# Another order of three engine queues in an attention stage of a fused graph-network kernel

## The reference, cut to what matters

```python
q2 = (q @ wiq.T + biq).reshape(N, H, D).transpose(1, 0, 2)      # N = 384, H = 16, D = 64
scores = jnp.einsum('hnd,hmd->hnm', q2, k2) * scale + mask[None]
attn = jax.nn.softmax(scores, axis=-1)
out = jnp.einsum('hnm,hmd->hnd', attn, v2)
x = x + out.transpose(1, 0, 2).reshape(N, OUT_F) @ wo.T + bo
```

## Time and profile before

| what | us |
|---|---|
| median of 3 runs | 937.59 (937.17, 937.59, 942.64) |
| the profiled execution, own time | 937.65 |
| its span, first to last instruction | 935.9 |
| attention: first transposes of head 0 to first product of the output projection | 225.05 to 295.47 |
| first product of relation 0 starts | 372.02 |
| TensorE's granted clock | 0.999 of full speed |

### The profile page before, as it was taken

How to read it: one execution, slowest core, us unless ns; L and a number is a source line. 1 busy time by engine, 2 the same in 40 slices (tenths; PEclk the granted TensorE clock), 3 DMA queues, 4 the chain that set the end, 5 groups by cost and what they waited for, 6 DMA issues and landing times.

```text
span 935.9 us, 13614 instructions
## 1 busy us (share of the span) xinstructions
PE 913.5 (98%) x4723; PEld 802.7 (86%) x4723; DVE 610.6 (65%) x1003; ACT 361.9 (39%) x568; POOL 489.6 (52%) x436
## 2 busy tenths in 40 slices
PE   5999999998999999999999999999999999999998
PEld 4999999997788887888888888888888888887886
DVE  6998888885886735656656565665646656434645
ACT  6433333344886334232223232323224345233532
POOL 5334444456676454757576575757685601320363
PEclk9999999999999999999999999999999999999999
DMA  8998756571337617453445535344333444333412
GB/s 204 243 278 223 228 155 154 153 195 2 52 43 206 161 20 257 110 171 98 142 114 167 150 113 157 104 149 113 92 110 122 157 130 136 118 107 90 136 45 90
DMA packets 89907, 128.60 MB, mean 137 GB/s; under 512 B 34480, under 2 KB 67456, under 8 KB 89856
## 3 DMA queue, kind: packets, MB, share of 16 engines
q1 hardware_dynamic: 72784, 123.54, 43.4%
q0 software_dynamic: 15552, 0.11, 4.2%
q10 hardware_dynamic: 1520, 4.30, 1.4%
HBM read 117.17 MB, written 7.59 MB: 133 GB/s over the span
## 4 chain that ended last, share of the span: by engine, by line
PE 89%; DMA 3%; DVE 3%; POOL 2%; issue 1%; ACT 1%; POOLq 0%; DVEq 0%; ACTq 0%
PE ps L672 47%; PE ps L471 18%; PE ps L746 8%; PE ps L515 4%; PE ps L635 4%; PE ps L595 2%; PE ps L551 2%; PE ps L538 2%; DMA raw<-in_L_gnn_weight 1%; DMA weight_d<-weight_sum,cell 1%; DVE wlo_all L1372 1%; DMA b_in<-in_L_gnn_biv 1%; PE ps L432 1%; POOL weight_d L1863 1%; POOL mean_lo L1842 1%
## 5 line engine op out<-in xcount | busy, mean ns | idle before, releaser
L1372 DVE TENSOR_TENSOR wlo_all<-raw,whi_all 128x1024 fp32r<-128x1024 f32 x120 | 199.3, 1669 | 121.6 <-ACT whi_all L960 121.5
L471 PE MATMUL ps<-acts,whi_all 128*128 128x384 f32 (+1 forms) x640 | 164.2, 337 | 0.0
L1842 POOL TENSOR_TENSOR mean_lo<-mean_f,mean_hi 128x384 fp32r<-128x384 f32 x76 | 88.6, 1165 | 119.6 <-ACT mean_hi L1110 119.3
L1110 ACT ACTIVATE mean_hi<-mean_f 128x384 fp32r<-128x384 f32 x76 | 39.9, 526 | 272.8 <-DVE mean_f L1539 272.8
L672 PE MATMUL ps<-whi_all,mean_hi 128*128 128x512 f32 x452 | 139.7, 390 | 2.5 <-POOL mean_lo L1842 2.5
L672 PE MATMUL ps<-wlo_all,mean_hi 128*128 128x512 f32 x452 | 139.3, 389 | 0.0
L672 PE MATMUL ps<-whi_all,mean_lo 128*128 128x512 f32 x452 | 139.2, 389 | 0.0
L960 ACT ACTIVATE whi_all<-raw 128x1024 fp32r<-128x1024 f32 x120 | 124.5, 1049 | 24.5 <-PE ps L672 18.0
L471 PEld LDWEIGHTS ps<-acts,whi_all 128*128 128x128 f32 x640 | 117.0, 190 | 0.1
L1863 POOL DMA_INDIRECT weight_d<-weight_sum,cell x48 | 95.5, 1989 | 31.5 <-DMA weight_d<-weight_sum,cell 18.6
L1810 POOL DMA_INDIRECT count_d<-met,cell x48 | 77.6, 1617 | 60.0 <-DMA count_d<-met,cell 46.8
(11 more groups left out here) (209 smaller groups left out, 1718.6 us busy)
## 6 DMA issues: line engine op xcount, KB each, us to landing
raw<-in_L_gnn_weight SPq DMA_DIRECT2D x64, 512.0 KB
rows_b<-rows_d SPq DMA_DIRECT2D x24, 384.0 KB, 5.2
raw<-in_L_gnn_w_gate SPq DMA_DIRECT2D x16, 512.0 KB
raw<-in_L_gnn_W_self SPq DMA_DIRECT2D x16, 512.0 KB
raw<-in_L_gnn_W_neigh SPq DMA_DIRECT2D x16, 512.0 KB
count_d<-total_r SPq DMA_DIRECT2D x8, 576.0 KB
rel_r<-count_d SPq DMA_DIRECT2D x8, 576.0 KB, 4.5
raw<-in_L_gnn_wq SPq DMA_DIRECT2D x32, 128.0 KB
```

The lines of the kernel that those rows point to most:

```text
L471: mm = pe.matmul(ps[:, j % 2, 0:N], stationary[j % RING][:, k, :], acts[:, a, moving, k, :], start=i == 0, stop=i == 3 * KT - 1)
L1110: act.activation(mean_of(q, k, 0)[:, 0, :], sums_of(q, k), ACT.Copy).then_inc(S["mean_hi"], 1)
L1372: dve.tensor_tensor(wlo_row[slot], raw[slot][:, :], whi_row[slot].bitcast(F32), ALU.subtract)\
L1842: pool.tensor_tensor(mean_of(q, k, 1)[:, 0, :], sums_of(q, k), mean_of(q, k, 0)[:, 0, :].bitcast(F32), ALU.subtract).then_inc(S["mean_lo"], 1)
```

## The change

It moves entries in the three hand-written queues and nothing else; no operation is added or removed, and no wait condition is changed. On PE the scores stand at the head of a step, `turn_probs(o, 0)` goes behind the third scores, and `turn_probs(o, 2)` behind `weigh_values(e)`. On ACT the exponentials of the next pair stand between the high copies in smaller groups, and `read_spread` and `pair_high` change places. On DVE the last maxima come earlier and `invert_sums` stands between the low parts. In the last step the tiles of `wo` take the corresponding places.

```diff
@@ -599,30 +599,29 @@
 
             for pair in range(H // 2):
                 e, o = 2 * pair, 2 * pair + 1
-                if pair:
-                    turn_probs(e, 0)
-                    turn_probs(e, 1)
                 if pair and o + 1 < H:
                     scores(pair + 1, 0)
                 if o + 1 < H:
                     scores(pair + 1, 1)
-                if o + 1 == H:
+                else:
                     turn_output(0)
                     turn_output(1)
                 if pair:
+                    turn_probs(e, 0)
+                    turn_probs(e, 1)
                     weigh_values(e - 1)
                 turn_probs(e, 2)
-                turn_probs(o, 0)
                 spread_sums(pair)
                 if o + 1 < H:
                     scores(pair + 1, 2)
                 else:
                     turn_output(2)
+                turn_probs(o, 0)
                 turn_probs(o, 1)
-                turn_probs(o, 2)
                 if o + 1 == H:
                     turn_output(3)
                 weigh_values(e)
+                turn_probs(o, 2)
             weigh_values(H - 1)
 
             def output_blocks(f, nt, blocks):
@@ -1056,27 +1055,28 @@
                 if pair and more:
                     exp(e + 2, 0)
                     exp(o + 2, 0)
+                if not more:
+                    column_high(0)
+                probs_high(e, 2)
                 if more:
                     exp(e + 2, 1)
+                    exp(o + 2, 1)
                 else:
-                    column_high(0)
                     column_high(1)
-                probs_high(e, 2)
                 probs_high(o, 0)
                 if more:
-                    exp(o + 2, 1)
+                    exp(e + 2, 2)
                 else:
                     column_high(2)
                 probs_high(o, 1)
+                if more:
+                    exp(o + 2, 2)
+                else:
+                    column_high(3)
                 probs_high(o, 2)
-                if not more:
-                    column_high(3)
-                if more:
-                    exp(e + 2, 2)
-                    exp(o + 2, 2)
-                read_spread(pair)
                 if pair:
                     pair_high(pair - 1)
+                read_spread(pair)
 
             act.wait_ge(S["probs_turned"], H * NT)
             act.dma_start(xres[:, :, :], x.rearrange("(t p) d -> p t d", p=P)).then_inc(S["x_in"], 16)
@@ -1460,29 +1460,31 @@
                     score_max(e + 2, 1)
                 if pair:
                     probs_low(e, 0)
-                    probs_low(e, 1)
                 if more:
                     score_max(o + 2, 1)
+                if pair:
+                    probs_low(e, 1)
                 if not more:
                     column_low(0)
-                    column_low(1)
                 if pair:
                     make_pair(pair - 1)
                 probs_low(e, 2)
+                if more:
+                    score_max(e + 2, 2)
+                    score_max(o + 2, 2)
+                else:
+                    column_low(1)
                 probs_low(o, 0)
                 if more:
-                    score_max(e + 2, 2)
+                    invert_sums(e + 2)
                 else:
                     column_low(2)
                 probs_low(o, 1)
                 if more:
-                    score_max(o + 2, 2)
+                    invert_sums(o + 2)
+                else:
+                    column_low(3)
                 probs_low(o, 2)
-                if not more:
-                    column_low(3)
-                if more:
-                    invert_sums(e + 2)
-                    invert_sums(o + 2)
 
             def last_pair_low(pair):
                 dve.wait_ge(S["pair_hi"], pair + 1)
```

## The result

The changed kernel takes 934.78 us (median of 20 runs, 932.97 to 936.1), the kernel before beside it 937.19 (20 runs, 936.12 to 943.52): ratio 0.9959, interval 0.9946 to 0.9972. It is about 2.4 us faster, inside the 1% that the prediction called no change, and 0.2 from the predicted 934.6. The profiled execution took 936.0, that is 1.2 above the median and the second longest of the 20, with a span of 934.2.

The account below looks back on a forecast made before the run. It took PE, busy 913.5 of 935.9 us, as the bound, with only idle time to win. Attention ends 2.1 us earlier (1.1 + 3.6 - 2.6); the count chain's advance of 3.0 gives 937.65 - 3.0 = 934.65, so 934.6; range 932.7 to 939.3.

Parts of the forecast that it names:

- The step (8.41 to 7.8): Middle steps 1 to 6 of attention: hidden PE waits go, gaining 0.6 us each, 3.6 us in all.
- The 0.1 for `turn_probs(o, 1)`: Middle steps: a new PE wait before this tile, whose buffer is not yet free, 0.07 to 0.16 us, taken as 0.1.
- The first step (1.1 earlier): First step of attention: the first weighing comes at 230.8 for 231.94, a gain of 1.1 us.
- The last step (15.65): Last weighing of step 6 to output projection: 15.65 us for 13.01, 2.6 lost, with three PE waits.
- The end of attention (293.4): Output projection starts at about 293.4 for 295.47, 2.1 us earlier (1.1 + 3.6 - 2.6).
- if ACT and DVE keep up: Condition for a 7.8 us step: ACT's busy 7.31 and DVE's 7.17 both lie below it.
- The advance of the count chain (S = 3.0): Behind attention: the last count's advance S sets the time won in the end, 3.0 us, between 1.1 and 4.3.
- Counts 30 and 31 fall into its end: Counts meet the end, not the start, of the burst of wo tiles and x reload, landing 3 to 4 us earlier.
- Rival one: Counts follow their own issue, not the burst, so the count chain advances only 1.1 us: 936.5; chance 0.25.
- What PE could use (2.1 + 2.2): Limit on the gain before relation 0: attention's 2.1 us plus PE's 2.2 us wait for the first mean, 4.3.
- Rival two: wo tiles meet counts POOL does not wait for during `pair_low`; count chain advances PE's full 4.3 us: 933.3; chance 0.15.
- Rival three (slower): ACT and DVE do not follow, steps stay 8.4 us, the last step still loses 2.6: 939.1; chance 0.12.

Follow-up runs that it names:

- after_nopair: The changed kernel with POOL's two `pair_low` operations left out for pairs 0 to 5, only the signal kept: 934.98 us, ratio 0.9968.
- early_w: The changed kernel with SP issuing relation 0's first two weight tiles ahead of its wait for the last count: 935.36 us, ratio 0.9959.
- pe_only: The kernel before with PE's new order alone, ACT and DVE keeping their old queues: 941.84 us, ratio 1.0049.
- actdve_only: The kernel before with the new orders of ACT and DVE alone, PE keeping its old queue: 952.42 us, ratio 1.0149.
- old_tail: The changed kernel with the last step of attention in the order of the kernel before on all three engines: 937.29 us, ratio 0.9981.
- new_tail_early: new_tail with SP also issuing relation 0's first two weight tiles ahead of its wait for the last count: 933.26 us, ratio 0.9953.
- before_early: The kernel before with SP issuing relation 0's first two weight tiles ahead of its wait for the last count: 937.53 us, ratio 0.9996.
- before_44: The kernel before with its last four counting transfers left out and not waited for: 937.23 us, ratio 0.9994.
- after_44: The changed kernel with its last four counting transfers left out and not waited for: 935.37 us, ratio 0.998.
- new_tail: The changed kernel with the last step of attention in a third order on PE, ACT and DVE: 939.66 us, ratio 1.001.

## Why the prediction was right, and where it was off

**The step (8.41 to 7.8): right, and a little too careful.** 7.70 to 7.73 in four of six steps, and in all six once POOL is out of the way (after_nopair) or no copy happens to be held (early_w, 7.72 to 7.74). The 0.1 for `turn_probs(o, 1)` did not come. pe_only and actdve_only show that the three orders are needed together.

**The first step (1.1 earlier): right.** From the wait's end at 228.54 to the first weighing at 230.70 it is 2.16, before 231.94 - 228.56 = 3.38: 1.2 won.

**The last step (15.65): right.** 15.46. The three waits were 0.7, 0.6 and 1.5 in the text and 0.74, 0.34 and 1.24 on the chip.

**The end of attention (293.4): off by 1.2.** It came at 294.62, 0.85 earlier than before instead of 2.1. The step that failed is "if ACT and DVE keep up": busy time of 7.17 for DVE was taken as what DVE needs, and a copy that stands still beside POOL's work was not in it. In this execution it cost 0.6 + 1.5 = 2.1 us; without these, attention would have ended near 292.5, and in early_w, which has the same attention and no copy held, it ended at 292.50. So with ACT and DVE keeping up the sum was even a little too careful. Which copies are hit is a matter of phase, that is of where a copy falls against POOL's queue in that execution: the kernel before has the copies elsewhere and was not hit, old_tail was hit lightly, new_tail_early three times.

**The advance of the count chain (S = 3.0): the size is open, the place was wrong.** Between the two profiled executions the tables moved by 0.97, but with the 2.66 by which the chain of after was late ahead of the first `pair_low` it is 3.63. Other profiles agree on the order of size and show the scatter: from count 17 to count 43 it took 91.6 to 95.9 in the three kernels with the old attention and all of `pair_low` (before, before_early, before_44), and 87.6 to 93.0 in the seven with the new steps. What failed is where it was to come from. "Counts 30 and 31 fall into its end" was to give 1.9 or more and gave 0.29: the wo tiles were issued 3.07 earlier (predicted 4.5), the counts 0.55, the reload of x 0.68, the next count 0.84. The stretch from count 17 to 28, priced at 1.1 for `pair_low`'s wait, gave 3.20: that wait of 1.09 is gone, and POOL also waited less for its counts to land (1.07 for 3.79), which the sum had at nothing. Why it waited less is not shown.

The page "DMA: Bandwidth & Descriptors" of the Trainium skill (section Queues, rings and completion order) made the tie to the burst worth nothing, and 0.29 is near that. But its turns packet by packet don't make these counts quick: beside the loads the next one still started 8.11 behind them, where it had been 8.40, and in early_w 5.55. How each transfer shared the DMA engines no run here shows.

Rival one's 936.5 for the profiled execution (936.0 taken) is then met by chance as well: its S = 1.1 was to be all that the change gives. Of the 1.64 by which relation 0 is earlier, 0.97 is S, 0.13 the issues between the tables and the first weight tile (352.20 for 353.30), and 0.54 that this tile's high part starts 9.1 behind its issue and not 9.6. These 0.67 I had not priced.

**So the forecast's number is nearer than its mechanism.** The median fell by 2.4, between the forecast's 3.0 and rival one's 1.1. That the forecast of 934.6 lies 0.2 from the median of 934.78 is in part luck: attention ended later than forecast, the counts gained elsewhere than forecast, and how far they run ahead or behind in an execution is set before the changed steps. The sizes behind the median are known only as far as one profile tells.

**What PE could use (2.1 + 2.2): wrong.** It took PE's visible wait for the mean as slack to be won. after_44, after_nopair and early_w show that the sums of the count planes take over at once: 1.59 to 1.60 in each, and 76.0 us from the output projection to relation 0, against 75.76 in after. Rival two's 933.3 was not to be had by the counts alone. (The 0.3 us of waits behind 372.02 were those for the mean; with the others it is 1.6. That changes nothing here, as both kernels take the same from there.)

**Rival three (slower): not seen, its premise wrong.** ACT and DVE followed. But new_tail shows a slower case that I had not named: attention finishes earlier than the count chain, PE stands, and beside the wait 2.8 us more are lost behind it, most of it at the low clock.

## What to carry to other kernels

Take a step of a busy engine apart start to start: that found 0.7 us a step which the busy time hid. Before pricing the gain, find the chain that decides the next stage's start, and then the gate behind that one; a stage made faster alone may only wait, and waiting can cost the clock as well. Where DVE copies inside SBUF while POOL works on two inputs there, look for held copies, in more than one execution: what a tuned order gains can hang on the phase. If ACT has time to spare, it can make the copy.

## What was not expected of the hardware

- A 0.29 us DVE copy lasted 0.66 to 2.22 us beside a POOL TENSOR_TENSOR with a row of 1.6 us, and ended 0.16 behind it each time. Beside POOL's TENSOR_SCALAR it did not. Copies of 0.48 to 0.55 without a TENSOR_TENSOR beside them (before, before_44, new_tail twice, early_w) each began 0.53 to 0.59 behind the start of a count's issue on POOL.
- POOL's sum of 128x384 took 1.02 alone and 1.99 and 1.85 beside DVE's TENSOR_TENSOR with both inputs in SBUF.
- The first operation of `pair_low` took 1.01 in one case of six before, and 1.57 to 1.61 in all six after. The longer rows start inside the row of the count's issue ahead of them: in all 72 such operations of twelve profiles the end lies 1.00 to 1.06 behind its own start or behind the end of that issue, whichever is later (260.82 + 1.61 = 262.43, and the issue ended at 261.39). So it is the same work of about 1.0, with up to 0.58 of waiting shown as busy.
- The same wait of PE, 1.96 to 2.03 us until 228.4 to 228.8, left the granted clock at 1.00 in eight profiles, and in five more it was 0.50 from 230 to 232. In new_tail it was 0.79 over the 12 us that hold the waits of 3.08 and 3.16 us, and 0.78 over the next 12, in which PE was full; the wait of 2.2 us in the kernel before left it at 1.00.
